# The products with the values laid between the query projection's products, two to each, one step later

## What is computed

```python
def _ada_ln(x, c, W_ss, b_ss):
    mu = jnp.mean(x, axis=-1, keepdims=True)
    var = jnp.mean((x - mu) ** 2, axis=-1, keepdims=True)
    h = (x - mu) / jnp.sqrt(var + EPS)
    ss = jax.nn.silu(c) @ W_ss + b_ss
    scale, bias = jnp.split(ss, 2, axis=-1)
    return (1.0 + scale)[:, None, :] * h + bias[:, None, :]
...
xq = _ada_ln(x_q, t_vec, Wss_q, bss_q)
xkv = _ada_ln(x_kv, t_vec, Wss_kv, bss_kv)
q = (xq @ Wq + bq).reshape(B, Lq, nh, dh)
kv = (xkv @ Wkv + bkv).reshape(B, Lkv, 2, nh, dh)
k = kv[:, :, 0]
v = kv[:, :, 1]
scores = jnp.einsum('bqhd,bkhd->bhqk', q, k) / jnp.sqrt(jnp.float32(dh))
attn = jax.nn.softmax(scores, axis=-1)
out = jnp.einsum('bhqk,bkhd->bqhd', attn, v).reshape(B, Lq, H)
return x_q + (out @ Wp + bp)
```

## Time and profile before

| | us |
|---|---|
| median of three runs | 1211.86 |
| lowest, highest | 1210.32, 1213.16 |
| profiled execution | 1211.32 |
| its span, first to last instruction | 1209.5 |

### The profile page before, as it was taken

How to read it: one execution, slowest core, us unless ns; L and a number is a source line. 1 busy time by engine, 2 the same in 40 slices (tenths; PEclk the granted TensorE clock), 3 DMA queues, 4 the chain that set the end, 5 groups by cost and what they waited for, 6 DMA issues and landing times.

```text
span 1209.5 us, 33685 instructions
## 1 busy us (share of the span) xinstructions
PE 1180.0 (98%) x11584; PEld 772.5 (64%) x11584; DVE 980.4 (81%) x2052; ACT 703.0 (58%) x1176; POOL 706.0 (58%) x948
## 2 busy tenths in 40 slices
PE   7799899999999999999999999999999999999997
PEld 2675666666666666666666666666666666666664
DVE  4787888888888888888888888888888888888875
ACT  1466556665656556665656565565656565565653
POOL 1553656657474756666575756666565656656434
PEclk9799999999999999999999999999999999999999
DMA  8110222332223232232323222323223222222222
GB/s 330 62 44 27 88 89 97 89 95 87 98 84 99 86 101 86 96 95 88 95 87 95 87 95 87 101 85 100 87 95 92 90 95 87 95 87 84 65 71 80
DMA packets 59866, 111.93 MB, mean 93 GB/s; under 512 B 6412, under 2 KB 6440, under 8 KB 59832
## 3 DMA queue, kind: packets, MB, share of 16 engines
q1 hardware_dynamic: 41400, 77.92, 21.2%
q10 hardware_dynamic: 18432, 33.56, 7.3%
HBM read 77.90 MB, written 33.55 MB: 92 GB/s over the span
## 4 chain that ended last, share of the span: by engine, by line
issue 46%; POOL 37%; POOLq 2%; DVE 0%; DVEq 0%
POOL xr L414 12%; POOL xh L381 7%; POOL w_lo L420 5%; POOL w_tmp L404 5%; POOL rstd L369 2%; POOL xr L390 2%; POOLq L221 2%; POOL nmv L365 2%; POOL veps L367 2%; POOL cur_sc L399 0%; POOLq L244 0%; POOLq L40 0%; POOLq L399 0%; DVE mv L812 0%; DVE oT_lo L827 0%
## 5 line engine op out<-in xcount | busy, mean ns | idle before, releaser
L553 ACT ACTIVATE q_hi<-ps_q,cur_bq 128x512 f16<-128x512 f32 x126 | 86.6, 687 | 268.0 <-PE ps_q L1113 230.6
L365 POOL TENSOR_TENSOR nmv<-mv,sign 128x2 f32<-128x2 f32 x128 | 27.0, 211 | 352.0 <-DVE mv L812 352.0
L820 DVE TENSOR_TENSOR xT_lo<-ps_t,xT_hi 128x512 f16<-128x512 f32 x128 | 88.5, 692 | 162.4 <-ACT xT_hi L494 162.4
L414 POOL TENSOR_TENSOR xr<-y,xr 128x512 f32<-128x512 f32 x128 | 163.1, 1275 | 46.1 <-ACT y L519 46.1
L390 POOL TENSOR_TENSOR xr<-xr,bp_row 128x512 f32<-128x512 f32 x128 | 163.1, 1274 | 13.1 <-POOL rstd L369 6.9
L876 DVE TENSOR_TENSOR pt_lo<-ps_t,pt_hi 128x512 f16<-128x512 f32 x256 | 164.7, 685 | 3.7 <-ACT pt_hi L543 3.5
L868 DVE TENSOR_TENSOR pr<-ps_s,mx 128x512 f32<-128x512 f32 x256 | 163.7, 681 | 0.0
L856 DVE TENSOR_REDUCE mx<-ps_s 128x8 f32<-128x512 f32 x256 | 158.8, 662 | 0.1
L494 ACT CAST xT_hi<-ps_t 128x512 f16<-128x512 f32 x128 | 75.0, 586 | 142.2 <-PE ps_t L1096 142.0
L584 ACT ACTIVATE pr<-pr,exp_scale 128x1024 f32<-128x1024 f32 x128 | 149.6, 1169 | 6.2 <-DVE pr L868 6.2
L543 ACT CAST pt_hi<-ps_t 128x512 f16<-128x512 f32 x256 | 136.3, 588 | 5.3 <-PE ps_t L1149 5.3
(11 more groups left out here) (160 smaller groups left out, 2323.7 us busy)
## 6 DMA issues: line engine op xcount, KB each, us to landing
x_in<-in_x_dram SPq DMA_DIRECT2D x128, 256.0 KB, 2.6
xr<-in_x_dram SPq DMA_DIRECT2D x128, 256.0 KB, 2.6
out_dram<-xr ACTq DMA_DIRECT2D x128, 256.0 KB, 2.2
raw<-in_L_xcond_Wss_kv_dram SPq DMA_DIRECT2D x4, 512.0 KB, 5.4
cx<-in_ctx_dram SPq DMA_DIRECT2D x1, 2048.0 KB, 12.4
raw<-in_L_xcond_Wss_q_dram SPq DMA_DIRECT2D x4, 512.0 KB, 13.4
raw<-in_L_xcond_Wkv_dram SPq DMA_DIRECT2D x2, 1024.0 KB, 15.7
wq<-in_L_xcond_Wq_dram SPq DMA_DIRECT2D x1, 1024.0 KB, 16.9
```

The costliest lines, as they stand in the source:

```text
L414: pool.tensor_tensor(xr[:, s, :], y[:, off % 2, :], xr[:, s, :], ALU.add).then_inc(y_ready, 1)
```

## The change

TensorE no longer has `weigh` at the end of a step. Its 24 products now stand between the 12 of `project`, two behind each, and they are those of unit u - 2, where before they were those of unit u - 1. VectorE's reciprocals and its normalising of o, of unit u - 2 as before, are put behind the maxima and the shift of unit u. ScalarE's `values` is put behind the exponential of the same step. GpSimd and SyncE keep their order. No instruction is added to or taken from any engine, apart from waits and registers.

```diff
             def step(b, i):
                 score(b, i)
-                project(b, i + 4)
+                for n in range(TERMS):
+                    project_part(b, i + 4, n)
+                    weigh_part(b, i - 2, 2 * n)
+                    weigh_part(b, i - 2, 2 * n + 1)
                 turn_p(b, i - 1)
                 project_out(b, i - 3)
                 turn_x(b, i + 8)
                 turn_o(b, i - 2)
-                weigh(b, i - 1)
...
+            def project_part(b, off, n, bank=ps_q, spare=0):
+
+                if not exists(b, off):
+                    return
+                s, m, k = (off // 4) % 2, off % 4, n % KC
+                if n == 0:
+                    if m == 0:
+                        wait(pe, xT_done, upto(b, off + 3))
+                    if off % PER < 4:
+                        wait(pe, w_done, KC * (b + off // PER) + m + 1)
+                    wait(pe, q_done, unit(b, off) - spare)
...
+            def weigh_part(b, off, n):
+
+                if not exists(b, off):
+                    return
+                pair, term = n // 3, n % 3
+                h, g = pair // 4, pair % 4
+                if n == 0:
+                    if off % PER == 0:
+                        wait(pe, vb_done, 4 * (b + off // PER + 1))
+                    wait(pe, o_done, 2 * unit(b, off))
+                if term == 0 and g == 0:
                     wait(pe, pt_done, 2 * unit(b, off) + h + 1)
...
-                denominators(b, i - 2)
                 score_max(b, i, 0)
                 score_max(b, i, 1)
+                softmax_shift(b, i)
+                denominators(b, i - 2)
                 normalise_o(b, i - 2)
-                softmax_shift(b, i)
...
-                if i == 1:
-                    values(b)
...
+                if i == 1:
+                    values(b)
                 if exists(b, i - 4):
```

More of the change, by code:

```diff
@@ L35, in adaln_cross_attention @@
     BH = 8
+    TERMS = 3 * KC
     MAX_SC, MAX_SH, MAX_B, LIMS = 4, 8, 12, 16
@@ L1097, in turn_x, with project @@
                 last.then_inc(xT_turned, 1)
-            def project(b, off, bank=ps_q, spare=0):
+            def project_part(b, off, n, bank=ps_q, spare=0):
                 if not exists(b, off):
                     return
-                s, m = (off // 4) % 2, off % 4
-                if m == 0:
-                    wait(pe, xT_done, upto(b, off + 3))
-                if off % PER < 4:
-                    wait(pe, w_done, KC * (b + off // PER) + m + 1)
-                wait(pe, q_done, unit(b, off) - spare)
-                cols = slice(P * m, P * (m + 1))
-                n = 0
-                for w, xt in ((w_hi, xT_hi), (w_hi, xT_lo), (w_lo, xT_hi)):
-                    for k in range(KC):
-                        last = pe.matmul(bank[:, :], w[:, k, cols], xt[:, s, k, :], start=(n == 0),
-                                         stop=(n == 3 * KC - 1))
-                        n += 1
-                last.then_inc(q_mm, 1)
+                s, m, k = (off // 4) % 2, off % 4, n % KC
[5 more added lines that the diff above has]
+                    wait(pe, q_done, unit(b, off) - spare)
+                w, xt = ((w_hi, xT_hi), (w_hi, xT_lo), (w_lo, xT_hi))[n // KC]
+                last = pe.matmul(bank[:, :], w[:, k, P * m:P * (m + 1)], xt[:, s, k, :], start=(n == 0),
+                                 stop=(n == TERMS - 1))
+                if n == TERMS - 1:
+                    last.then_inc(q_mm, 1)
+            def project(b, off, bank, spare):
+                for n in range(TERMS):
+                    project_part(b, off, n, bank, spare)
             def score(b, off):
@@ L1152, in turn_p @@
                     last.then_inc(p_turned, 1)
-            def weigh(b, off):
+            def weigh_part(b, off, n):
                 if not exists(b, off):
                     return
-                if off % PER == 0:
-                    wait(pe, vb_done, 4 * (b + off // PER + 1))
-                wait(pe, o_done, 2 * unit(b, off))
-                for h in range(2):
-                    wait(pe, pt_done, 2 * unit(b, off) + h + 1)
-                    for g in range(4):
-                        pair = 4 * h + g
-                        dst = ps_v[:, h, 2 * VC * g:2 * VC * (g + 1)]
-                        for n, (pt, part) in enumerate(((pt_hi, 0), (pt_hi, 1), (pt_lo, 0))):
-                            last = pe.matmul(dst, pt[:, pair, :],
-                                             vb[:, part, 2 * g + h, :, :].rearrange("p h c -> p (h c)"),
-                                             start=(n == 0), stop=(n == 2))
+                pair, term = n // 3, n % 3
[5 more added lines that the diff above has]
+                if term == 0 and g == 0:
+                    wait(pe, pt_done, 2 * unit(b, off) + h + 1)
+                pt, part = ((pt_hi, 0), (pt_hi, 1), (pt_lo, 0))[term]
+                last = pe.matmul(ps_v[:, h, 2 * VC * g:2 * VC * (g + 1)], pt[:, pair, :],
+                                 vb[:, part, 2 * g + h, :, :].rearrange("p h c -> p (h c)"),
+                                 start=(term == 0), stop=(term == 2))
+                if g == 3 and term == 2:
                     last.then_inc(pv_mm, 1)
```

## The result

The changed kernel takes 1227.41 us (median of four runs, 1225.68 to 1229.54); the kernel before, run beside it, 1212.51 (four runs, 1210.32 to 1213.38). The ratio is 1.0127, with a 95% interval of 1.0103 to 1.0150: 15.4 us slower, between 12.5 and 18.2. A few single executions of these kernels ran at a far lower granted clock from end to end (one of an experiment took 1524.13 us at 0.75 of full speed); they are left out of every figure. The forecast was 1221.2, and the upper end of its range 1227.0. The sign and the main mechanism were right; the amount was some 6 us too small, and the time lies 0.4 us outside the range.

A forecast was written before the change was run, and what follows sets the result against it. TensorE, busy 98% of the span, was taken to bound the kernel alone. Stalls of +10.2 us less 0.9 at the loop's edge gave +9.3, so 1221.2 us from a median of 1211.86; range 1215.5 to 1227.

The forecast's parts named there:

- Part 2, the stalls: Query projection's first product waits for xT: 0.25 us late at i = 0, 0.44 at i = 4, +10.2 us in all.
- Rival (b): No stall at xT, turn_x ending early enough or the wait being met: 1211.0 us, no change; chance 0.05.
- Part 4, the loop's edge: At the loop's branch TensorE no longer waits for queued small products: 13 edges of about 0.07 us, -0.9 us.
- Part 1, the products: TensorE's products in the new order: small ones at 30 ns already hide their loads, nothing lost or gained, zero.
- a plain step of 8.54: Sign set for TensorE's steps at i = 1, 2, 3, 5, 6, 7: 8.54 us; another value would fail part 1.
- (c): Rival: each change between wide and small products on TensorE costs 10 ns, +32 us, 1253; chance 0.08, also in part.
- (a): Rival: small products get cheaper between wide ones on TensorE, 3.5 us, so 1217.7, at most 6.9 us; chance 0.10.
- Part 3, VectorE and ScalarE: Work moved on the other engines costs nothing: VectorE keeps 1.3 us idle, the copies of v 0.45 spare.
- rival (d): VectorE or ScalarE falls behind in step 2, where 0.45 is spare: 0.3 us x 15 more, 1225.7; chance 0.05.
- Part 4, start and end: One group of small products, 0.73 us, off the path at the start, one onto it at the end: zero, ±0.7.
- a later wait: Upper bound of the i = 4 wait for xT, 0.54 us instead of 0.44: 1.4 us more, in the range's upper end.

The follow-up runs named there:

- the kernel before with this move alone: Kernel before, with only its 24 small products, whole and of unit u - 1, moved ahead of turn_x and turn_o: 1232.29 us, ratio 1.0180.
- block and interleaved order: Block: changed kernel with its 24 small products as one block behind the query projection, 1225.77 us, ratio 1.0122. Interleaved: the changed kernel itself.

## Why the prediction was off

**Part 2, the stalls: right in place, number and size.** Forecast 0.25 at i = 0 and 0.44 at i = 4, 28 or so times; measured 0.259 and 0.434, 29 times between 150 and 1180 us. The sum of 10.2 stands (14 x 0.434 + 16 x 0.259). The sum over the cover (1.94 to make xT, 1.75 left) was right because both sides were read from starts of one and the same step, and the two forms of the wait (on the product, or on a register instruction ahead of it) were told apart. Rival (b), no stall, is out.

**Part 4, the loop's edge: right.** Forecast -0.9, measured some -0.95; the step i = 7 is now like the others (8.566). The reason given, that the branch had to wait for the queued small products, fits: every order without them at the end loses the 0.9, also the kernel before with this move alone (8.569 at i = 7, as in the plain steps). That it is the queue that holds the branch back, no run tested by itself.

**Part 1, the products: the first step that failed.** It says that "where products follow on transposes or transposes on products, in the same rows, nothing is lost at all". Those rows show transposes behind products of 512 columns. The change puts them behind a product of 66 columns, and there 0.03 is lost, in every step: some 3.7 us, where the sum has zero. This row didn't exist before, and I had taken the nearest one for it without a bound of its own, although the order showed the new neighbours. The test that the prediction set itself, a plain step of 8.54, gave 8.57. The rest of the part held: between the wide products a small one still takes 29 to 35 ns until the next product starts (704.92, 704.95, 704.98 above), and 12 wide and 24 small take 704.98 - 701.66 = 3.32 us where 3.33 was forecast. So the 10 ns at each change of (c) don't exist, and (a) has next to nothing to gain: block and interleaved order differ by 0.08 us over the whole kernel.

What is behind the 0.03 is argued, not shown. The loads of TensorE's weights from 150 to 1180 us, after (busy us, mean ns of one, idle before):

```profile
L1170 PEld LDWEIGHTS ps_v<-vb,pt_hi 128*128 128x128 f16 x1910 | 168.1, 97 | 111.8
L1152 PEld LDWEIGHTS ps_t<-ident,pr 128*128 128x128 f32 x960 | 102.8, 140 | 0.0
...
L1112 PEld LDWEIGHTS ps_q<-xT_hi,w_lo 128*128 128x128 f16 x480 | 46.8, 98 | 0.0
```

A float32 load lasts 140 ns, a float16 one 97. In the step shown, the first load for the transposes starts at 704.95, 0.03 ahead of its transpose; in the step of the earlier trace rows it starts at 693.27, 0.22 ahead, beside a wide product. The 0.141 between the first two transposes is about a float32 load's length. So it may be that the loads get no lead behind a small product. But float16 loads of 97 ns keep up with products 29 ns apart, so the length of a load doesn't decide it alone, and no run changed the load's type. The Trainium skill, "TensorE: Matmul & The Clock Gate", section "Weight-path perf modes — Fast Weight Load (FWL) and DoubleRow", has the faster loading of weights on for 128 of them of any type but FP32. The trace agrees in so far as the float32 loads are the longer ones. The rule of the same page of the Trainium skill in section "Back-to-back issue gap", which the prediction weighed, is not borne out at the 66 columns here: 29 to 35 ns for a pair of load and small product, between wide products too, where the rule has 81 at 128 columns.

**Part 3, VectorE and ScalarE: right in the loop, and the second step that failed in the start.** VectorE's step came out as worked through: first maximum at 702.75 - 700.44 = 2.31 (forecast 2.31), shift at 3.48 (3.46), reciprocals at 4.68 (4.66), idle 1.26 before xT_lo (1.3). pt_lo came at 5.92 instead of 5.60 and waited 0.19 for pt_hi, since this is a step whose projection is 0.44 late; turn_o still had room. No wait for o or pt_lo appears, so rival (d) is out. But the sum has both moves at nothing, and I had worked them through only for the steps of the loop. In batch 0 TensorE waits for VectorE anyway, and there VectorE's order costs 1.26 and the copies 1.46, 2.72 together. The first is waiting for pt_lo. The second came with a lower granted clock and not with more waiting, a way to lose time that the prediction doesn't name. In the changed kernel itself, putting `values(0)` back takes 2.56 off the start.

**Part 4, start and end: right as far as the traces tell.** "One group off the path and one onto it: zero." With the small products moved and the other two engines as before, the start is 0.74 shorter. From the last unit's scores to the end it is 25.22 in the changed kernel and 24.48 in the kernel before, 0.74 longer. Both are a group's length of 0.73. At the end this rests on the sum alone: with VectorE in its old order the same move made the whole end 1.42 longer (76.49 against 75.07), and the new order took 0.61 of it back, so part of the agreement there may be luck.

The errors together: 3.7 + 2.7 = 6.4, and 9.3 + 6.4 = 15.7, where the traces have 15.71. Both had the same sign, and the range had 5.8 of room above the forecast, kept for a later wait and for rival (d), neither of which came.

## What to carry to other kernels

Before moving work, look at two places: what the work was covering where it stood (here 0.73 us of cover went, with 0.54 to spare), and what will stand directly beside it where it goes, since a price read behind one neighbour doesn't hold behind another. And work the start and the end through as separate cases: an edit that is free in a loop paced by one engine (VectorE's new order here) costs time where that engine waits for another. A start has to be read with its granted clock beside it, or a slower clock is taken for waiting. Putting the same work directly ahead of the product that waits, instead of directly behind it, would have cost nothing that these timings can tell.

## What the runs showed of the hardware

- Eight float32 transposes directly behind a product of 66 columns take 0.90 us until the next product may start, four take 0.47; behind a product of 512 columns it is 0.87 and 0.44. One such neighbourhood costs 0.03 us, all of it between the first transpose and the second (0.141 instead of 0.109), as kernels that differ in it show.
- Small and wide float16 products can be mixed freely: 12 wide and 24 small take 3.326 us in pairs and 3.327 as two blocks (medians), and over the whole kernel pairs and two blocks differ by 0.08 us.
- Some 0.07 us were lost at each pass of the hardware loop when 24 small products were queued ahead of the branch (0.96 in 13 passes in the kernel before, 0.13 in the first), and none when the float32 transposes were.
- TensorE's granted clock fell in the start behind stretches in which TensorE had waited: to 0.58 of full speed from 124 to 128 us in the kernel before, and in the changed kernel in the windows below (us, busy time and instructions of PE, PEld, DVE, ACT and POOL, granted clock, DMA share, GB/s).

```profile
124.00:128.00 4.00, 2.08 (x29) 1.57 (x29) 3.03 (x5) 3.23 (x8) 1.85 (x3) 0.84 0.00 0
128.00:132.00 4.00, 4.00 (x34) 2.24 (x34) 3.28 (x6) 2.24 (x3) 1.51 (x3) 0.74 0.00 0
132.00:136.00 4.00, 1.78 (x18) 1.31 (x14) 3.97 (x10) 2.70 (x4) 3.23 (x4) 1.00 0.86 292
136.00:140.00 4.00, 4.00 (x42) 2.49 (x42) 3.73 (x7) 1.69 (x3) 0.78 (x3) 0.62 0.28 106
```

The stretch around the whole start, in the kernel before, the changed kernel and the one with `values(0)` at its old place:

```profile
110.00:155.00 45.00, 40.29 (x411) 26.45 (x410) 38.60 (x75) 25.19 (x41) 23.88 (x36) 0.96 0.19 65
110.00:155.00 45.00, 39.09 (x356) 24.46 (x354) 35.53 (x66) 23.88 (x38) 21.74 (x31) 0.92 0.18 60
110.00:155.00 45.00, 39.95 (x407) 25.20 (x406) 38.34 (x73) 24.75 (x40) 23.87 (x36) 0.96 0.22 65
```

A value such as 0.62 is a mixture of the clock's two levels, 1.2 and 2.4 GHz, within the window. The changed kernel fell to the lower level twice in the start, the other two once. The mean over the start is 0.92 in each of the six kernels that have the small products out of step 1 and the late copies, and 0.96 in each of the seven others. What makes the second fall come or stay away is open.
